# Cross attention on one core: the product G x of batches 1 to 31 by seven block products instead of eight, with the block sums of x made by accumulating DMAs

## What is computed

```python
x_q = jnp.einsum('oc,bcn->bno', w_qk, y)
x_k = jnp.einsum('oc,bcn->bon', w_qk, x)
x_v = jnp.einsum('oc,bcn->bon', w_v, x) + b_v[None, :, None]
energy = jnp.einsum('bnc,bcm->bnm', x_q, x_k)
attention = jax.nn.softmax(energy, axis=-1)
attention = attention / (1e-07 + attention.sum(axis=1, keepdims=True))
x_r = jnp.einsum('bcn,bnm->bcm', x_v, attention)
x_r = jax.nn.relu(jnp.einsum('oc,bcn->bon', w_t, x - x_r) + b_t[None, :, None])
return x + x_r
```

## Time and profile before

| what | us |
|---|---|
| median of 3 runs | 1847.62 (1847.48 to 1848.41) |
| the profiled execution's span | 1846.8 |
| TensorE matmuls busy | 1841.7 (100%) |
| VectorE busy | 1499.5 (81%) |
| ScalarE busy | 1310.9 (71%) |
| GpSimd busy | 788.0 (43%) |
| DMA queue of SyncE, share of 16 engines | 15.8% |

### The profile page before, as it was taken

How to read it: one execution, slowest core, us unless ns; L and a number is a source line. 1 busy time by engine, 2 the same in 40 slices (tenths; PEclk the granted TensorE clock), 3 DMA queues, 4 the chain that set the end, 5 groups by cost and what they waited for, 6 DMA issues and landing times.

```text
span 1846.8 us, 26440 instructions
## 1 busy us (share of the span) xinstructions
PE 1841.7 (100%) x8901; PEld 1553.5 (84%) x8901; DVE 1499.5 (81%) x2034; ACT 1310.9 (71%) x1799; POOL 788.0 (43%) x422
## 2 busy tenths in 40 slices
PE   9999999999999999999999999999999999999999
PEld 8888888888888888888888888888888888888887
DVE  7878787787887877878878788787787877878777
ACT  7767776677666786667776677766677666776665
POOL 5543344432444424444244452444533444334431
PEclk9999999999999999999999999999999999999999
DMA  3201111011110111101111111111011110111101
GB/s 108 68 25 57 58 68 68 23 68 46 68 68 23 68 46 68 68 33 58 46 68 68 48 43 46 68 68 61 30 48 66 68 68 23 64 50 68 68 1 46
DMA packets 34090, 101.92 MB, mean 55 GB/s; under 512 B 4224, under 2 KB 5248, under 8 KB 34048
## 3 DMA queue, kind: packets, MB, share of 16 engines
q1 hardware_dynamic: 33760, 101.07, 15.8%
q10 hardware_dynamic: 288, 0.39, 0.1%
HBM read 67.90 MB, written 33.55 MB: 55 GB/s over the span
## 4 chain that ended last, share of the span: by engine, by line
PE 98%; DVE 1%; ACT 0%; issue 0%; POOL 0%; DVEq 0%; ACTq 0%; POOLq 0%
PE pv L796 37%; PE row_b L691 19%; PE row_a L691 14%; PE pv L768 9%; PE row_b L754 5%; PE row_a L754 5%; PE row_a L745 5%; PE row_b L745 5%; DVE colsum L536 0%; PE pv L898 0%; PE pv L754 0%; PE pv L931 0%; PE pv L902 0%; ACT p_sb L336 0%; DVE z_lo L503 0%
## 5 line engine op out<-in xcount | busy, mean ns | idle before, releaser
L218 POOL TENSOR_TENSOR y_lo<-y_raw,y_hi 128x896 fp32r<-128x896 f32 (+1 forms) x128 | 277.1, 2190 | 546.7 <-ACT y_hi L297 357.1
L543 DVE SCALAR_TENSOR_TENSOR p_lo<-p_sb,row_inv,p_hi 128x1024 fp32r<-128x1024 f32 x254 | 325.4, 1282 | 96.0 <-ACT p_hi L344 95.9
L327 ACT ACTIVATE ev<-row_b 128x512 f32<-128x512 f32 x384 | 229.5, 598 | 199.7 <-PE row_b L691 199.1
L203 POOL TENSOR_TENSOR x_lo<-x_sb,x_hi 128x1024 fp32r<-128x1024 f32 x63 | 152.2, 2415 | 449.2 <-ACT x_hi L280 449.2
L336 ACT ACTIVATE p_sb<-p_sb,neg_max 128x1024 f32<-128x1024 f32 x256 | 295.1, 1154 | 28.6 <-DVE neg_max L518 24.6
L344 ACT ACTIVATE p_hi<-p_sb,row_inv 128x1024 fp32r<-128x1024 f32 x256 | 292.4, 1143 | 30.7 <-PE pv L796 30.0
L536 DVE SCALAR_TENSOR_TENSOR colsum<-p_sb,row_inv,colsum 128x1024 f32<-128x1024 f32 x224 | 291.7, 1302 | 8.5 <-DVE row_inv L526 0.6
L796 PE MATMUL pv<-p_hi,z_hi 128*128 128x512 f32 x1024 | 273.7, 389 | 0.0
L796 PE MATMUL pv<-p_hi,z_lo 128*128 128x512 f32 x1024 | 273.7, 389 | 0.0
L518 DVE CUSTOM_DVE_ANT_0 p_sb<-row_a,ev 128x1024 f32<-128x1024 f32 x128 | 156.6, 1223 | 143.6 <-PE row_a L691 143.6
L796 PE MATMUL pv<-p_lo,z_hi 128*128 128x512 f32 (+1 forms) x1047 | 271.7, 383 | 0.0
(11 more groups left out here) (157 smaller groups left out, 3585.9 us busy)
## 6 DMA issues: line engine op xcount, KB each, us to landing
x_sb<-x SPq DMA_DIRECT2D x64, 512.0 KB, 4.6
out<-res SPq DMA_DIRECT2D x62, 512.0 KB, 3.4
y_raw<-y SPq DMA_DIRECT2D x64, 256.0 KB, 3.7
y_raw<-y SPq DMA_DIRECT2D x32, 512.0 KB, 3.7
out<-res SPq DMA_DIRECT2D x2, 256.0 KB, 2.1
res<-w_qk SPq DMA_DIRECT2D x1, 256.0 KB, 3.0
res<-w_t_T SPq DMA_DIRECT2D x1, 256.0 KB, 6.7
res<-w_v SPq DMA_DIRECT2D x1, 256.0 KB, 7.8
```

Of the source, the lines that this page charges most:

```text
L218: nc.gpsimd.tensor_tensor(y_lo[:, of:, cols], y_raw[:, 1 + of:8, cols], y_hi[:, of:, cols].bitcast(FP32), ALU.subtract).then_inc(y_lo_done, 1)
L327: nc.scalar.activation(ev[:, to, :], bank_b, ACT.Copy, scale=scale).then_inc(b_copied, 1)
L543: nc.vector.scalar_tensor_tensor(out=p_lo[r][:, :], in0=p_sb[r][:, :], scalar=row_inv[:, j:j + 1], in1=p_hi[r][:, :].bitcast(FP32), op0=AL ...
```

## The change

G x of batches 1 to 31 is made by the same kind of scheme as the energy: seven products of three matmuls. The operands are G's blocks and four sums of them, made once in batch 0 (`g_operands` on GpSimd, `g_operands_high` on ScalarE), and x's blocks and four sums of them, T1 to T4. These sums are made by DMA: SyncE loads four blocks of x to `xt_raw`, and GpSimd issues three DMAs that add to them (xt_one, xt_two, xt_four). ScalarE makes their high parts (`xt_high`, at t = 2 and 3), GpSimd their low parts (`xt_low`, behind both x_low). The seven products stand between the pv passes of pair 3. Partial banks are passed on by ScalarE (`gx_pass`, four times a batch), and VectorE adds two of them (`gx_add`). One pv pass of pair 3 moves ahead of the last product. x_sb is now one buffer, loaded by keep_x for `finish`; x for the split is loaded a second time to x_raw, which lies where x_lo does. There is no turn_buf: `turn` writes to p_sb 0, ahead of p_low(3,1), and the spread factors go to colsum. x_bias runs at t = 1 and 2 instead of 0 and 1, z_low 0 ahead of scale 1, y_high 3 ahead of the high parts of the last two blocks. GpSimd's batches are written out instead of looped.

```diff
--- before.py
+++ after.py
...
+        def sb_again(first, name, shape):
+            with nc.sbuf_tensor(first, shape, FP32) as raw:
+                pass
+            return raw, sb(name, shape, FP32R)
...
@@ -155,7 +171,14 @@
         @block.sync
         def _(sp):
             def load_x(b, par, kt):
-                sp.dma_start(x_sb[par][:, kt, :], x_dram[b][:, kt, :]).then_inc(x_in[kt], DMA)
+                sp.dma_start(x_raw[par][:, kt, :], x_dram[b][:, kt, :]).then_inc(x_in[kt], DMA)
+
+            def keep_x(b, kt):
+                sp.dma_start(x_sb[:, kt, :], x_dram[b][:, kt, :]).then_inc(x_kept[kt], DMA)
+
+            def load_xt(b):
+                for block, kt, cols in ((X_T1, 0, left), (X_T3, 1, right), (X_T2, 1, right), (X_T4, 1, left)):
+                    sp.dma_start(xt_raw[:, block, :], x_dram[b][:, kt, cols]).then_inc(xt_in, DMA)
 
             def load_y(b):
                 sp.dma_start(y_raw[:, 0, :], y_dram[b][:, 0, BANK:N]).then_inc(y_in, DMA)
@@ -172,15 +195,22 @@
                     sp.wait_ge(y_hi_done, NP * (b + 1))
                     sp.wait_ge(y_lo_done, NP * (b + 1))
                     load_y(b + 1)
+                    if not first:
+                        sp.wait_ge(gx21_full, b)
+                    load_xt(b + 1)
                 for t in range(KT):
                     if not first:
                         store(b - 1, t)
-                    if not last:
-                        load_x(b + 1, 1 - par, t)
+                        keep_x(b, t)
+                if not last:
+                    if not first:
+                        sp.wait_ge(w_done, KT * b)
+                    for kt in range(KT):
+                        load_x(b + 1, 1 - par, kt)
 
             sp.dma_start(wqk_sb, by_channel(w_qk)).then_inc(wqk_in, DMA)
             for kt in range(KT):
-                load_x(0, 0, kt)
+                keep_x(0, kt)
             load_y(0)
             sp.dma_start(wtT_sb, by_channel(w_t_T)).then_inc(weights_in, DMA)
             sp.dma_start(wv_sb, by_channel(w_v)).then_inc(weights_in, DMA)
...
             def x_low(b, par, kt):
                 pool.wait_ge(x_hi_done, KT * b + kt + 1)
-                nc.gpsimd.tensor_tensor(x_lo[par][:, kt, :], x_sb[par][:, kt, :],
-                                        x_hi[par][:, kt, :].bitcast(FP32), ALU.subtract).then_inc(x_lo_done, 1)
+                raw = x_raw[par][:, kt, :] if b > 0 else x_sb[:, kt, :]
+                nc.gpsimd.tensor_tensor(x_lo[par][:, kt, :], raw, x_hi[par][:, kt, :].bitcast(FP32),
+                                        ALU.subtract).then_inc(x_lo_done, 1)
+
+            def xt_one(b):
+                pool.wait_ge(xt_in, 4 * DMA * b)
+                shared = x_dram[b][:, 0, right].rearrange("p (a n) -> p a n", a=1).to_broadcast([P, 2, BANK])
+                pool.dma_start(xt_raw[:, X_T1:X_T3 + 1, :], shared,
+                               accum_op=ALU.add).then_inc(xt1_added, DMA)
+
+            def xt_two(b):
+                pool.wait_ge(xt1_added, DMA * b)
+                pool.dma_start(xt_raw[:, X_T2, :], xt_raw[:, X_T1, :],
+                               accum_op=ALU.add).then_inc(xt2_added, DMA)
+
+            def xt_four(b):
+                pool.wait_ge(xt2_added, DMA * b)
+                pool.dma_start(xt_raw[:, X_T4, :], xt_raw[:, X_T2, :],
+                               accum_op=ALU.add).then_inc(xt4_added, DMA)
+
+            def xt_low(b, h):
+                pool.wait_ge(xt_hi_done, 2 * (b - 1) + h + 1)
+                two = slice(2 * h, 2 * h + 2)
+                nc.gpsimd.tensor_tensor(xt_lo[:, two, :], xt_raw[:, two, :],
+                                        xt_hi[:, two, :].bitcast(FP32), ALU.subtract).then_inc(xt_lo_done, 1)
+
...
@@ -231,10 +301,17 @@
 
             def batch(b, par, last=False):
                 if not last:
+                    xt_one(b + 1)
                     y_sums(b + 1)
+                    xt_two(b + 1)
+                    if b == 0:
+                        g_operands()
                     y_low(b + 1, 0)
+                    xt_four(b + 1)
                     for kt in range(KT):
                         x_low(b + 1, 1 - par, kt)
+                    for h in range(2):
+                        xt_low(b + 1, h)
                     pool.wait_ge(p_lo_done, NT * (b + 1))
                     for t in range(1, NP):
                         y_low(b + 1, t)
...
-                act.wait_ge(x_in[kt], DMA * (b + 1))
+                act.wait_ge(x_in[kt], DMA * b)
                 if not early:
                     act.wait_ge(w_done, KT * (b - 1))
-                nc.scalar.activation(x_hi[par][:, kt, :], x_sb[par][:, kt, :], ACT.Copy).then_inc(x_hi_done, 1)
...
+            def xt_high(b, h):
+                if h == 0:
+                    act.wait_ge(xt1_added, DMA * b)
+                else:
+                    act.wait_ge(xt4_added, DMA * b)
+                two = slice(2 * h, 2 * h + 2)
+                nc.scalar.activation(xt_hi[:, two, :], xt_raw[:, two, :],
+                                     ACT.Copy).then_inc(xt_hi_done, 1)
+
+            def x_bias(b, kt):
+                act.wait_ge(x_kept[kt], DMA * (b + 1))
+                nc.scalar.activation(x_sb[:, kt, :], x_sb[:, kt, :], ACT.Identity,
                                      bias=bias[:, kt:kt + 1]).then_inc(x_biased, 1)
 
...
+            def g_operands_high():
+                for of, to in ((g_hi, gs_hi), (g_lo, gs_lo)):
+                    nc.scalar.activation(to[:, G_N11, :], of[:, 0, 0:P].bitcast(FP32), ACT.Copy,
+                                         scale=-1.0).then_inc(gs_copied, 1)
+                    nc.scalar.activation(to[:, G_12:G_22 + 1, :],
+                                         of[:, 1, :].bitcast(FP32).rearrange("p (j c) -> p j c", j=2),
+                                         ACT.Copy).then_inc(gs_copied, 1)
+                act.wait_ge(g_summed, 5)
+                nc.scalar.activation(gs_hi[:, G_S1:G_NS4 + 1, :], g_sums, ACT.Copy).then_inc(gs_hi_done, 1)
+
+            def gx_pass(b, to, of, done, count, scale):
+                act.wait_ge(done, count)
+                nc.scalar.activation(to, of, ACT.Copy, scale=scale).then_inc(gx_passed, 1)
 
...
                     y_high(1, 1)
-                if t < 2 and not first and (t == 1 or not last):
-                    x_bias(b, par, t)
-                if t == 0 and last:
+                if 0 < t < 3 and not first and (t == 2 or not last):
+                    x_bias(b, t - 1)
+                if t == 1 and last:
                     x_bias_last()
                 exponent(b, t, 0)
                 exponent(b, t, 1)
@@ -399,6 +511,10 @@
                     y_high(b + 1, 1)
                 if t == NP - 1 and last:
                     p_scaled(b, t, 0)
+                if t == NP - 1 and not last:
+                    gx_pass(b + 1, gx11, gx22, gx22_part, 3 * b + 1, -1.0)
+                    gx_pass(b + 1, ev[:, 3, :], gx12, gx12_part, b + 1, 1.0)
+                    gx_pass(b + 1, ev[:, 2, :], gx22, gx22_part, 3 * b + 2, 1.0)
                 if t == NP - 1:
                     p_high(b, t, 1, first)
                 if t == NP - 1 and last:
...
@@ -408,22 +524,27 @@
                 for t in range(NP):
                     pair(b, par, t, first, last=last)
                 if not last:
+                    gx_high_one(b + 1)
+                    gx_pass(b + 1, gx21, gx22, gx22_part, 3 * b + 3, -1.0)
                     y_high(b + 1, 2)
-                    gx_high(b + 1)
+                    y_high(b + 1, 3)
+                    gx_high_two(b + 1)
                     t_high(b + 1, 0)
                     if first:
                         act.wait_ge(setup_dve, 5)
...
@@ -470,10 +591,20 @@
                                                      in1=hnT_hi[:, :, :].bitcast(FP32), op0=ALU.mult,
                                                      op1=ALU.subtract))
 
+            def gx_add(b):
+                dve.wait_ge(gx12_full, b)
+                dve.wait_ge(gx_passed, 4 * b - 1)
+                nc.vector.tensor_tensor(gx12, gx12, ev[:, 2, :], ALU.add).then_inc(gx_added, 1)
+                dve.wait_ge(gx_passed, 4 * b)
+                nc.vector.tensor_tensor(gx22, gx22, ev[:, 3, :], ALU.add).then_inc(gx_added, 1)
+
             def gx_parts(b, first=False):
                 b_low(b, 0, B_11, row_b[:, left], 1)
                 dve.wait_ge(neg_b11_made, b + 1)
-                dve.wait_ge(g_done, 4 * b + 2)
+                if first:
+                    dve.wait_ge(g_done, 2)
+                else:
+                    dve.wait_ge(gx_added, 2 * b)
                 nc.vector.tensor_tensor(t_raw[:, T_1, :], row_b[:, right], neg_b11[:, :],
                                         ALU.add).then_inc(t_made, 1)
...
@@ -549,10 +684,16 @@
 
             def turn(b):
                 dve.wait_ge(acc_done, NT * (b + 1))
```

(88 more changed lines are left out.)

125 lines of the change are left out of this document (87 added, 38 removed).

## The result

| | before | after |
|---|---|---|
| median, us | 1847.6 | **2082.66** (2079.07 to 2089.32) |
| profiled span, us | 1846.8 | 2077.7 |
| mean granted clock of TensorE | 1.00 | 0.961 |

The ratio is 1.1277, interval 1.1255 to 1.13: the changed kernel is 12.8% slower, 107.7 us above the forecast of 1975 and above the range. The direction was right, the size was not.

The account below looks back on a forecast made before the run. TensorE, with 98% of the chain, was taken to bound the kernel. 1846.8 - 21.1 for removed matmuls + 31 x 4.19 (129.9) for waits + 19 for the start = 1974.6 profiled, median 1975 us; range 1930 to 2025.

Parts of the forecast that it names:

- rival C: A 3.5 us wait drops TensorE's clock to 1.2 GHz: +3.4 us per batch, 2080 in all; chance 0.06.
- the start: In batch 0, ScalarE's g_operands_high waits for GpSimd, so exponent(0,0) is 20 us later: +19 us once, bounds 14 to 26.
- z_low: Ahead of p1, ScalarE's late z_high and then z_lo end after TensorE wants p1: 0.2 us of wait per batch.
- Matmuls removed: G x in seven products of three instead of 24 matmuls on TensorE: 0.68 us less per batch, 21.1 in all.
- gx_p5's wait: TensorE waits at gx_p5 for GpSimd's xt_low, which alternate with VectorE's column sums: 3.54 us per batch.
- Rival A: No collision, GpSimd and VectorE overlap freely: +2.27 us per batch, 1937 in all; chance 0.15.
- gx_p4's wait: TensorE waits at gx_p4 for ScalarE's pass 4, queued behind p_high(3,1), neg_b11 and gx_hi: 0.45 us per batch.
- GpSimd's issues at 0: GpSimd's time to issue the accumulating DMAs falls in its idle stretches and costs 0; 1 us each is in the range.
- Rival B: VectorE's 0.3 us before Z gives way, or accumulating DMAs hold GpSimd up: 2006 or 2037; chance 0.17.
- Rival D: Faster: xt_low ready when gx_p5 is reached, pass 4 in time, the start overlapped: 1826.5; chance 0.05.
- its half: Of Rival D, only xt_low being ready when gx_p5 is reached holds: 1859.5, slower still; chance 0.05.

Follow-up runs that it names:

- run 1: The changed kernel with 15 added useless matmuls ahead of gx_p5's wait for the sums' low parts: 2027.14 us, ratio 1.0974.
- run 8: The kernel before, without the change, with GpSimd repeating y_low(b+1,0) twice behind x_low 1: 1921.27 us, ratio 1.0396.
- run 5: The changed kernel with the orders of run 2, run 3 and run 4 together, and gx_pass 4 ahead of neg_b11 and gx_hi on ScalarE: 1938.82 us.
- run 4: The changed kernel with y_sums ahead of xt_one in GpSimd's queue: 2057.85 us, ratio 1.1135.
- run 3: The changed kernel with GpSimd making G's sums ahead of y_sums and the first xt_one, and ScalarE splitting them a pair later: 2056.19 us.
- run 2: The changed kernel with xt_low 0 ahead of x_low 1 on GpSimd, and gx_p5 waiting for xt_low 0 alone: 1966.17 us, ratio 1.0648.
- run 7: Run 6 with VectorE instead of GpSimd making the low parts of xt 0 and x's second block: 1858.6 us, ratio 1.0055.
- run 9: Run 7 with y_high 3 behind gx_high_two on ScalarE: 1850.48 us, ratio 1.0018.
- run 6: Run 5 with xt_high 0 at t = 1, both x_high at t = 2 and xt_low 1 last: 1914.78 us, ratio 1.0361.

## Why the prediction was wrong, point by point

**The range and rival C.** The main step that failed is the clock: the sum has no term for it, it got a chance of 0.06 as a rival, and it cost 1.9 us per batch, 58 in all. I wrote that "no row of before shows such a fall". But no row of before shows a wait of 3.5 us either: the longest there is 1.1 us, once, so the trace could not speak against it. The Trainium skill, TensorE: Matmul & The Clock Gate, section "Why this matters for your kernels", which advises against such gaps between bursts of matmuls, was the only evidence, and the runs agree with it (run 1). Since C's condition was my own forecast (a wait of 3.5 us), its chance should have been near that of the forecast. C's price was 3.4 us per batch and came out at 1.8 to 1.9: no row of before gave its 15 matmuls at the low clock, and even in the batch shown, with 6.8 us of low clock, there are 13, as part of the low stretch passes in the wait. That 2080 hit the median is luck in part: C was too dear by some 47 us, and three smaller terms that I had at too little (time around waits, a pv pass, the start; some 50 us together, below) made up for it.

**What the 107.7 us are.** 58 the clock, some 31 the time around waits, 14 the wait of a pv pass, 4.5 the start, less 6 for z_low; and the profiled execution lies 5.0 us under the median where I had taken 0.8, which makes 4 more. About 2 us stay open.

**Matmuls removed**, -0.68: as predicted, 93 matmuls fewer by the page (8901 to 8808), 31 x 3.

**gx_p5's wait**: 3.54 forecast, 3.50 measured as idle time. I had worked it out from start to start; by that measure it is 3.68 (above), still close. The alternation is there as written: the two xt_low end 5.68 us after x_lo, 5.74 forecast. The collision is shown by itself in run 8. Rival A, no collision, is refuted.

**gx_p4's wait**: 0.45 forecast, 0.49 measured as idle time; run 5 removed it by the order of ScalarE alone.

**z_low**: 0.2 forecast, none measured. TensorE was later than forecast, so ScalarE had time.

**Not in the sum: time around a wait.** About 1.0 us per batch. I took it that TensorE resumes at 0.227 per matmul; behind a wait at full clock the second matmul comes 0.11 us later than that, and the profile's idle time leaves out another 0.16 of each wait. 0.28 us per wait explains some 0.8 of the 1.0 here, 17 of the 19 us beside the waits in run 8, and most of the ten us too many in run 4. That it is a term per wait is my reading of these three; no run varied it by itself.

**GpSimd's issues at 0**: wrong. I placed the accumulating DMAs in idle stretches by looking at what waits for them, not at what is queued behind them. xt_one, ahead of y_sums, waits for a load and takes 1.2 us to issue; a pv pass pays 0.46 us (the waits), and run 4 gives back 24.8 us in all. The DMAs themselves land in 5.4 and 6.2 us and fit, as forecast. By the Trainium skill, DMA: Bandwidth & Descriptors, section "Anatomy of one DMA", 512 KB would take an estimated 3.2 us; 5.4 were measured, which changes nothing here. The "2 MB more a batch" left out what xt_one reads: the page's HBM reads rose from 67.90 to 149.16 MB, 2.6 MB a batch.

**The start**: 19 forecast, 23.5 measured in the trace and 26.5 by run 3, about the upper bound of 26. The changed kernel's timeline of it, ScalarE and GpSimd:

```profile
46.92 0.63 ACT L387 ACTIVATE gs_hi<-res 128x512 fp32r<-128x512 f32 x1 [21.11 <-POOL res L271]
47.46 1.14 ACT L445 ACTIVATE p_sb<-p_sb,neg_max 128x1024 f32<-128x1024 f32 x1
...
36.33 1.35 POOL L240 DMA_DIRECT2D xt_raw<-x  x1 [7.72 <-DMA xt_raw<-x]
```

GpSimd waits for the load until 36.33, and ScalarE stands for 21.1 us behind the sums of G. exponent(0,0) moved by 22.4 us (20.4 forecast), and the granted clock is 0.50 from 35 to 50 us and 0.56 from 50 to 55: the first matmuls behind TensorE's wait of 21.9 us run at the low level too.

**Rival B** (VectorE's margin of 0.3 us ahead of Z) does not show in the changed kernel, because the longer waits ahead hide it. It appeared as soon as these were removed: 1.16 us in run 2, 1.87 in run 5.

**Rival D** and its half: gx_p5 in time (runs 2, 5, 7) did not bring 1826.5. Even in run 9, with hardly any idle time left in steady state, the batch is only 0.26 us shorter than before, not 0.68. Of the other 0.42, some 0.26 are VectorE again: its last gx_lo ends at 1049.41 and Z starts at 1049.47, 0.16 us after it could by the pace of the matmuls ahead (and its second matmul is 0.10 late too). The list of waits doesn't show it, because the matmul ahead still counts as busy. Where the last 0.16 go is not shown.

## What to carry to other kernels

Where a forecast contains a wait of a few us on a TensorE that never idled, price the clock with it, and for every wait the overlap lost ahead of it and the late second matmul behind it (0.28 us here); the absence of a clock fall in a trace without waits says nothing. A GpSimd instruction with two SBUF inputs added beside VectorE's is paid by VectorE: count what it lies on, and ask whether VectorE can do it itself, as in run 7. For an instruction that is moved or added on a queue, look at what stands behind it, not only at who needs it. And take the time of a steady batch apart from the start: run 9 gains in the one and loses it in the other.

## What the runs showed of the hardware that I had not expected

- The granted clock fell in 29 of 31 batches after a wait of 3.5 us (in run 4 in all 31), in 14 of 31 after one of 1.9, and in none after waits of 1.2 to 1.3 (runs 2 and 8, where single ones reach 1.3 and 2.1). In run 6 it fell four times in steady state, in four of the eight places where a wait of 1.2 to 2.0 us and one of 1.1 us stood 1.2 us apart. It stayed low for 3.4 or 6.8 us. In some batches the fall began during the wait, in others over 1 us after TensorE was back at work.
- VectorE and GpSimd do not always alternate. Column sums got in between two xt_low (3.03 and 3.17 us), yet one p_low was held through three GpSimd instructions in a row (8.55 us). What decides which remains open; it was not tried.
- Issuing a DMA takes GpSimd itself 0.83 to 1.35 us.
